# Graph network kernel on one core: source one-hots compared on VectorE, edge-term steps spread singly, features turned early

## The chip, the cores and the metric

The program runs on one core of one Trainium2 chip. The metric is the device time of one execution in microseconds (us), the median over several runs. Names of engines: TensorE (PE, matmuls; PEld is its weight loads), VectorE (DVE), ScalarE (ACT), GpSimd (POOL) and SyncE (SP), which here only issues DMAs.

## The reference, cut to what matters

Four graph layers over 128 nodes with 512 features, each followed by a residual and a layer norm. Only the first two matter here.

```python
# layer 0: attention over the edges, then a feed-forward
h1 = layer_norm(x + attn_out @ Wo + bo)
ff = relu(h1 @ W1 + b1) @ W2 + b2
x  = layernorm(x + layer_norm(h1 + ff))
# layer 1: 4096 edges
edge_feat = concatenate([x[src], x[dst], edge_attr])      # 4096 x (512 + 512 + 64)
h         = mish(edge_feat @ W1 + b1)
messages  = mish(h @ W2 + b2)
agg       = segment_sum(messages, dst, 128)
```

`src` and `dst` are 4096 integers below 128, `edge_attr` is 4096 x 64.

## The kernel before, in words

Every engine has its own instruction stream, written out by hand; semaphores join them. Nothing is scheduled by a tool, so the order in the code is the order on each engine.

The layer-1 product is split. The features of source and destination are first multiplied by W1 per node (128 rows, called Ahi/Alo and Bhi/Blo), and then spread to the edges by a matmul with a one-hot matrix: ST (source) and DT (destination), both 128 nodes x 4096 edges. The third part, `edge_attr @ Wc`, is the edge term: 16 steps, each of two banks of 512 edges, six matmuls (L483) and two evictions on ScalarE (L281) into C. Steps 0 to 11 are the ring steps: they use the four PSUM banks of PRE in turn, so step s waits until ScalarE has evicted step s - 2. Steps 12 to 15 come later, between the matmuls of the first layer (L605).

DT and ST are made in the same way: VectorE compares ids with a row of numbers into Dbf and Sbf (edges on partitions, L825), TensorE turns four tiles of 128 x 128 into a bank (`turn_onehots`, L458), and ScalarE copies the bank out (`onehot_out`, L295), eight groups each. These banks are the same ring as those of the edge term, counted by `pre_done` and `pre_read`. The edge features `ea` are turned too (`turn_features`, L465), in four groups, split into a high part (ScalarE, L313) and a low part (VectorE, L835).

Order of TensorE around the change: scores, values, edge counts; the attention product (L531), Wo (L427, bank1 and bank2), the eight DT groups, the turn of the normed node features (L410), the first feed-forward F1 in four blocks (L436) with two ST groups after each, the second feed-forward F2 (L427) in two halves of six and a last part of four, with edge steps 0, 1-2 and 3-5 between them, then steps 6 to 10, the turn of the next node features (L410), step 11, and the per-node products with W1 (L584 to L589). From there VectorE and ScalarE serve the long edge loop (L605, L622, L632), which is unchanged.

SyncE issues the loads in a fixed order, all on one queue; some wait for a semaphore, because tensors share places in SBUF. VectorE between F1 and the next norm: low part of W1 (L878), `features_low(3)`, two copies of the turned graph matrices (L881, L882), two adds (L885, L887), and then `residual` (L771), which waits for F2's last matmuls and starts a chain of norms that ends with `nx_ready` (L792).

Of the kernel before, what the change touches and what calls it, by code (L numbers as in the profile page):

```python
# [13 lines left out]
N = 128  # L14
D = 512
# [25 lines left out]
def gnn_kernel(nc, a, out):  # L41

    ctx = ExitStack()
    with ctx:
# [33 lines left out]
        def overlay(*spots):  # L78

            made = {}  # L80
            with ExitStack() as st:
                end = 0
                for name, place, units, dt in sorted(spots, key=lambda s: s[1]):
                    if place > end:
# [10 lines left out]
                        ("W1raw", 64, 8, F32), ("EAThi", 72, 4, F32R), ("Wchi", 76, 1, F32R), ("Wc", 77, 1, F32), ("ffT", 78, 2, F32),  # L95
                        ("rows", 80, 7, F32), ("EATlo", 91, 4, F32R))
        other = overlay(("Dbf", 28, 4, BF16), ("Sbf", 52, 4, BF16), ("W1hi", 56, 8, F32R), ("W1lo", 64, 8, F32R),
                        ("Wclo", 77, 1, F32R), ("xhi", 78, 1, F32R), ("xlo", 79, 1, F32R))
        low = overlay(("Clo", 0, 32, F32R), ("Mlo", 64, 4, F32R))
        last = overlay(("W3", 0, 8, F32), ("W4", 8, 4, F32), ("WsR", 12, 4, F32), ("WnR", 16, 4, F32),  # L100
                       ("WsT", 32, 4, F32), ("WnT", 36, 4, F32), ("uT", 40, 1, F32), ("aggT", 41, 1, F32), ("agg_sb", 42, 1, F32),
# [4 lines left out]
        def chunks(v, k):  # L106
            return v.rearrange("p (c n) -> p c n", c=k)
# [11 lines left out]
        C = edge["C"].rearrange("p (g j e) -> p g j e", g=G, j=KC)  # L119
        Hlo, Mlo = low["Clo"].rearrange("p (g j e) -> p g j e", g=G, j=KC), chunks(low["Mlo"], GT)  # L120
        ST, DT = edge["ST"], edge["DT"]
        W2hi, W2lo = chunks(edge["W2hi"], KC), chunks(edge["W2lo"], KC)
        Hhi = edge["Hhi"].rearrange("p (b j e) -> p b j e", b=2, j=KC)
        M, Mhi = chunks(edge["M"], GT), chunks(edge["Mhi"], GT)
# [22 lines left out]
        def quarter(b, j):  # L147
            return b[:, P * j:P * (j + 1)]
# [9 lines left out]

        DT_UNIT, ST_UNIT, C_UNIT = 0, G, 2 * G
        RING_STEPS = KC * (PAIRS - 1)
        UNITS = C_UNIT + 2 * RING_STEPS
        LATE_BANKS = ((bank[3], bank[4]), (bank[1], bank[2]))

        S = {}
        for name in ("x_in ids_in vecs_in ea_in wq_in0 wq_in1 wk_in0 wk_in1 wv_in wo_in f1_in f2_in w1_in wc_in w2_in w3_in w4_in g_in ws_in wn_in b1g_in "
                     "out_stored consts ident_ready ident_bf_ready x_transposed xT_ready cols_done cols_ready q_done k_done v_done "
                     "qk_ready v_ready onehot_bf ct_done ct_read uniform_ready eighth ea_done ea_hi ea_lo wc_hi wc_lo scores_done s_centred exp_done attn_ready ao_done ao_ready wo_done "
                     "stat_ready rstd_ready nx_ready nT_done nT_ready f1_done ff_ready f2_done pre_done pre_read late_done late_read "  # L170
                     "xw_ready w2_hi w2_lo w1_hi w1_lo xs_hi xs_lo ab_done ab_ready "
                     "graphT_ready graphT_done graph_ready deg_ready dinv_ready "
                     "z1_done z1_read h_hi h_lo z2_done z2_read m_hi m_lo m_oh agg_done "
                     "agg_ready aggT_done aggT_ready u_done u_ready o_done "
                     "g0_done g0_ready g1_done g1_ready g2_done g2_ready g3_done nm_done nm_ready l3_done wt_done wt_ready y_final "
                     "dve_chain").split():
            S[name] = sem(name)
# [4 lines left out]
        def w_view(w):  # L182
            return w.rearrange("(c p) n -> p c n", p=P)
# [16 lines left out]
        def _(sp):  # L200
# [13 lines left out]
            for name in EARLY_ROWS[2:4]:  # L214
                load_row(name)
            sp.dma_start(F1, w_view(a["L0_gnn_W1"])).then_inc(S["f1_in"], 16)
            for name in EARLY_ROWS[4:]:
                load_row(name)
            sp.dma_start(W1raw, w_view(a["L1_gnn_W1"][0:2 * D, :])).then_inc(S["w1_in"], 16)

            sp.wait_ge(S["pre_done"], ST_UNIT)
            sp.wait_ge(S["ct_done"], 1)
            sp.dma_start(F2, w_view(a["L0_gnn_W2"])).then_inc(S["f2_in"], 16)
            sp.wait_ge(S["pre_done"], C_UNIT)
            sp.dma_start(W2raw, w_view(a["L1_gnn_W2"])).then_inc(S["w2_in"], 16)


# [42 lines left out]
        def _(act):  # L270
# [22 lines left out]
            def onehot_out(dst, unit, g):  # L293
                act.wait_ge(S["pre_done"], unit + g + 1)
                act.activation(dst[:, GE * g:GE * (g + 1)], PRE[(unit + g) % 4][:, :], ACT.Copy).then_inc(S["pre_read"], 1)  # L295

            def edge_term_out(steps):

                for s in steps:
                    q, j = s // KC, s % KC  # L300
                    for o in range(2):
                        k = 2 * s + o
                        if s < RING_STEPS:
                            act.wait_ge(S["pre_done"], C_UNIT + k + 1)
                            src, signal = PRE[(C_UNIT + k) % 4], "pre_read"
                        else:
                            act.wait_ge(S["late_done"], k - 2 * RING_STEPS + 1)
                            src, signal = LATE_BANKS[s % 2][o], "late_read"
                        bias_out(C[:, 2 * q + o, j, :], src[:, :], "L1_gnn_b1", j).then_inc(S[signal], 1)
# [32 lines left out]
            for i in range(4):  # L342
                w1_high(i)
                relu_out(i)
                onehot_out(ST, ST_UNIT, 2 * i)
                onehot_out(ST, ST_UNIT, 2 * i + 1)
            features_high(3)
            edge_term_out(range(RING_STEPS))
            act.wait_ge(S["w2_in"], 16)
            act.activation(W2hi[:, :, :], W2raw, ACT.Copy).then_inc(S["w2_hi"], 1)  # L350
            edge_term_out(range(RING_STEPS, RING_STEPS + 1))

# [43 lines left out]
        def _(pe):  # L396
# [64 lines left out]
            def turn_features(q):  # L461

                for i in range(GT):
                    t = tile_of(2 * q, i)
                    done = nc.tensor.transpose(quarter(EA_BANKS[q], i), flat(ea[:, t:t + 2, :]), ident[:, :])  # L465
                done.then_inc(S["ea_done"], 1)
# [58 lines left out]
            pe.wait_ge(S["uniform_ready"], 1)  # L525
            for j in range(KC):
                mm(quarter(bank[3], j), v_sb[:, P * j:P * (j + 1)], uniform[:, :], start=j == 0, stop=False)
            for o, j in ((o, j) for o in range(2) for j in range(KC)):
                h = 2 * j + o
                pe.wait_ge(S["attn_ready"], o + 1)  # L530
                done = mm(bank[3][HEAD * o:HEAD * (o + 1), P * j:P * (j + 1)], v_sb[:, HEAD * h:HEAD * (h + 1)], attn[:, o, j, :],  # L531
                          start=False, stop=j == KC - 1)
            done.then_inc(S["ao_done"], 1)
            pe.wait_ge(S["ea_in"], 16)
            turn_features(0)
            pe.wait_ge(S["wo_in"], 16)
            for h in range(2):
                pe.wait_ge(S["ao_ready"], h + 1)
                for b in range(2):
                    done = columns_by((bank[1], bank[2]), aoT, Wo, b, (2 * h, 2 * h + 1), None, KC - 1)  # L540
                    if h == 1:
                        done.then_inc(S["wo_done"], 1)
            pe.wait_ge(S["ident_bf_ready"], 1)
            pe.wait_ge(S["cols_ready"], 1)
            pe.wait_ge(S["ct_read"], 1)
            turn_onehots(Dbf, DT_UNIT, range(G))
            pe.wait_ge(S["ea_lo"], 1)
            turn_features(1)
            transpose_halves((bank[1], bank[2]), y, S["nx_ready"], 0, S["nT_done"])
# [3 lines left out]
            for i in range(4):  # L553
                if i >= 2:
                    pe.wait_ge(S["ea_lo"], 3)
                features_by(F1_BANKS[i], 2 * i, (2 * i, 2 * i + 1), F1, xT, KC, S["f1_done"])
                turn_onehots(Sbf, ST_UNIT, (2 * i, 2 * i + 1))
            pe.wait_ge(S["ff_ready"], FC - 2)
            turn_features(3)
            pe.wait_ge(S["wc_lo"], 1)  # L560
            edge_term(range(1))
            pe.wait_ge(S["f2_in"], 16)
            columns_by((bank[1], bank[2]), ffT, F2, 0, range(FC - 2), 0, FC - 1)
            edge_term(range(1, 3))
            pe.wait_ge(S["graphT_ready"], 2)
            pe.wait_ge(S["ff_ready"], FC)
            nc.tensor.transpose(bank[4][:, 0:N], Ahat[:, :], ident[:, :])
            nc.tensor.transpose(bank[4][:, N:2 * N], Cn[:, :], ident[:, :]).then_inc(S["graphT_done"], 1)
            columns_by((bank[1], bank[2]), ffT, F2, 1, range(FC - 2), 0, FC - 1)
            edge_term(range(3, 6))  # L570
            for h in range(2):
                columns_by((bank[1], bank[2]), ffT, F2, h, range(FC - 2, FC), 0, FC - 1).then_inc(S["f2_done"], 1)

            edge_term(range(6, RING_STEPS - 1))
            pe.wait_ge(S["graph_ready"], 2)
            transpose_halves((bank[3], bank[4]), xs, S["nx_ready"], 2, S["nT_done"])
            edge_term(range(RING_STEPS - 1, RING_STEPS))
# [59 lines left out]
            def turn(q):  # L637
# [5 lines left out]
                    done = nc.tensor.transpose(quarter(TURN[q % 4], k), w[:, k, P * (q % KC):P * (q % KC + 1)], ident[:, :])  # L643
                done.then_inc(S["wt_done"], 1)

            pe.wait_ge(S["ab_ready"], 2)
            first_layer(0, range(3), range(2))
            pe.wait_ge(S["ab_ready"], 6)
# [92 lines left out]
        def _(dve):  # L741
# [91 lines left out]
            def features_low(q):  # L833
                dve.wait_ge(S["ea_hi"], q + 1)
                v.tensor_tensor(EATlo[:, q, :], EA_BANKS[q][:, :], EAThi[:, q, :].bitcast(F32), ALU.subtract).then_inc(S["ea_lo"], 1)  # L835
# [40 lines left out]
            for c in range(2 * KC):  # L876
                dve.wait_ge(S["w1_hi"], c // 2 + 1)
                v.tensor_tensor(W1lo[:, c, :], W1raw[:, c, :], W1hi[:, c, :].bitcast(F32), ALU.subtract).then_inc(S["w1_lo"], 1)  # L878
            features_low(3)
            dve.wait_ge(S["graphT_done"], 1)  # L880
            v.tensor_scalar(Ahat[:, :], bank[4][:, 0:N], small[:, 2:3], None, ALU.mult).then_inc(S["graph_ready"], 1)  # L881
            v.tensor_copy(Cn[:, :], bank[4][:, N:2 * N]).then_inc(S["graph_ready"], 1)  # L882

            dve.wait_ge(S["nx_ready"], 2)
            chain(v.tensor_tensor(xw[:, :], y[:, :], r("L0_gnn_b2"), ALU.add))  # L885
# [142 lines left out]
```

## Time and profile before

| | |
|---|---|
| median of 3 runs | 248.84 us (248.77 to 249.32) |
| the profiled execution | 250.41 us, its span 248.6 us |
| TensorE busy | 233.4 us (94%) |
| VectorE busy | 154.0 us (62%) |
| ScalarE busy | 121.5 us (49%) |
| chain that ended last | PE 82%, DVE 5%, DMA 4%, ACT 4%, issue 2% |

The span counts from the first to the last instruction of the profile; the rest of the profiled execution lies around it. Busy shares are means over stages: here the stretch from 21 to 84 us is what the change touches, and the long edge loop after it (84 to 208 us) keeps TensorE busy without a break.

### The profile page before, as it was taken

What the parts mean: (1) busy time and instruction counts of PE and PEld (TensorE: products, weight loads), DVE (VectorE), ACT (ScalarE), POOL (GpSimd) and SP (SyncE); (2) the same over time, 40 slices, a digit from 0 to 9 for tenths busy, and PEclk for the clock granted to TensorE, in tenths of its full rate; (3) what the DMA queues carried; (4) which work ended last, traced back from release to release, by engine and by line L of the source; (5) the groups of instructions that cost most, each with busy time, mean ns of one, the idle gap of its engine ahead of it and who ended that gap; (6) DMA issues with size and microseconds to landing.
All of it is one profiled execution on the core that took longest, in us unless ns stands there. A gap on an engine that the chain in (4) does not pass through costs nothing.

```text
span 248.6 us, 3285 instructions
## 1 busy us (share of the span) xinstructions
PE 233.4 (94%) x1269; PEld 187.8 (76%) x1269; DVE 154.0 (62%) x266; ACT 121.5 (49%) x221; POOL 5.5 (2%) x17
## 2 busy tenths in 40 slices
PE   7989999998999999999999999999999998999980
PEld 3866779765676788888888888888888887986760
DVE  2959774535669756775855848758567456174724
ACT  0325189857938953654735546456356341260000
POOL 0000000000000000000000000000000000010001
PEclk9999999999999999999999999999999999999997
DMA  7999977400381000008122050040000000000001
GB/s 212 297 400 407 411 261 273 169 4 0 114 255 55 0 0 0 3 0 298 40 80 91 0 170 4 8 161 0 0 3 0 0 0 3 0 0 3 0 0 44
DMA packets 12991, 23.39 MB, mean 94 GB/s; under 512 B 920, under 2 KB 3888, under 8 KB 12848
## 3 DMA queue, kind: packets, MB, share of 16 engines
q1 hardware_dynamic: 12336, 22.81, 25.9%
q10 hardware_dynamic: 640, 0.37, 0.6%
q8 instruction: 10, 0.16, 0.3%
q14 instruction: 5, 0.04, 0.0%
HBM read 22.92 MB, written 0.26 MB: 93 GB/s over the span
## 4 chain that ended last, share of the span: by engine, by line
PE 82%; DVE 5%; DMA 4%; ACT 4%; issue 2%; SPq 1%; POOL 0%; POOLq 0%; DVEq 0%
PE bank L622 33%; PE bank L605 12%; PE bank L427 9%; PE bank L436 6%; DMA Wk<-in_L_gnn_Wk 4%; PE bank L483 4%; PE bank L632 3%; PE bank L633 3%; ACT C L281 2%; PE bank L416 1%; PE bank L643 1%; PE bank L446 1%; PE bank L458 1%; PE bank L410 1%; ACT DT L295 1%
## 5 line engine op out<-in xcount | busy, mean ns | idle before, releaser
L622 PE MATMUL bank<-W2hi,Hhi 128*128 128x512 f32 x128 | 49.8, 389 | 0.0
L622 PE MATMUL bank<-W2lo,Hhi 128*128 128x512 f32 x128 | 49.8, 389 | 0.0
L622 PE MATMUL bank<-W2hi,Clo 128*128 128x512 f32 x128 | 49.8, 389 | 0.0
L365 ACT ACTIVATE Mhi<-M 128x512 fp32r<-128x512 f32 x32 | 20.2, 632 | 45.4 <-DVE M L932 45.4
L937 DVE TENSOR_TENSOR Mlo<-M,Mhi 128x512 fp32r<-128x512 f32 x32 | 22.1, 689 | 24.4 <-ACT M L366 24.4
L932 DVE TENSOR_TENSOR M<-bank,b2r 128x512 f32<-128x512 f32 x32 | 22.0, 687 | 12.7 <-PE bank L633 7.6
L622 PEld LDWEIGHTS bank<-W2lo,Hhi 128*128 128x128 f32 x128 | 24.0, 188 | 5.0
L622 PEld LDWEIGHTS bank<-W2hi,Clo 128*128 128x128 f32 x128 | 24.0, 188 | 5.0
L622 PEld LDWEIGHTS bank<-W2hi,Hhi 128*128 128x128 f32 x128 | 24.0, 188 | 5.0
L358 ACT ACTIVATE Hhi<-C 128x512 fp32r<-128x512 f32 x32 | 20.0, 624 | 12.4 <-DVE C L918 12.1
L918 DVE TENSOR_TENSOR C<-bank,C 128x512 f32<-128x512 f32 x32 | 21.4, 689 | 5.1 <-PE bank L605 4.1
L923 DVE TENSOR_TENSOR Clo<-C,Hhi 128x512 fp32r<-128x512 f32 x32 | 22.0, 687 | 3.7 <-ACT C L359 3.6
L281 ACT ACTIVATE C<-bank,cols 128x512 f32<-128x512 f32 x32 | 19.7, 693 | 9.2 <-PE bank L483 9.2
L605 PE MATMUL bank<-ST,AB 128*128 128x512 f32 x64 | 20.0, 399 | 0.0
L359 ACT ACTIVATE C<-C 128x512 f32<-128x512 f32 x32 | 19.8, 618 | 0.0
L366 ACT ACTIVATE M<-M 128x512 f32<-128x512 f32 x32 | 19.7, 616 | 0.0
L605 PE MATMUL bank<-DT,AB 128*128 128x512 f32 x64 | 19.4, 390 | 0.0
L605 PEld LDWEIGHTS bank<-ST,AB 128*128 128x128 f32 x64 | 11.6, 188 | 3.9 <-DVE C L918 1.0
L605 PEld LDWEIGHTS bank<-DT,AB 128*128 128x128 f32 x64 | 12.0, 188 | 2.6
L632 PE MATMUL bank<-Mhi,Dg 128*128 128x512 f32 x32 | 12.6, 395 | 0.7 <-DVE Mlo L937 0.7
L633 PE MATMUL bank<-Mlo,Dg 128*128 128x512 f32 x32 | 12.5, 389 | 0.0
L446 PE MATMUL bank<-ident 128*128 128x512 bf16 x26 | 8.4, 466 | 1.6 <-DVE ident L819 1.6
(178 smaller groups left out, 316.9 us busy)
## 6 DMA issues: line engine op xcount, KB each, us to landing
F<-in_L_gnn_W SPq DMA_DIRECT2D x2, 2048.0 KB, 13.4
W1raw<-in_L_gnn_W SPq DMA_DIRECT2D x1, 2048.0 KB, 17.6
W<-in_L_gnn_W SPq DMA_DIRECT2D x1, 2048.0 KB, 9.2
Wq<-in_L_gnn_Wq SPq DMA_DIRECT2D x2, 512.0 KB, 5.8
Wk<-in_L_gnn_Wk SPq DMA_DIRECT2D x2, 512.0 KB, 9.7
Wv<-in_L_gnn_Wv SPq DMA_DIRECT2D x1, 1024.0 KB, 12.7
ea<-in_edge_attr SPq DMA_DIRECT2D x1, 1024.0 KB, 12.6
Wo<-in_L_gnn_Wo SPq DMA_DIRECT2D x1, 1024.0 KB, 15.7
```

The source lines that it names most:

```text
L281: return act.activation(dst, src, func, bias=cols[:, col[name] + j:col[name] + j + 1])
L358: act.activation(Hhi[:, g % 2, j, :], C[:, g, j, :], ACT.Mish)
L365: act.activation(Mhi[:, t, :], M[:, t, :], ACT.Mish)
L427: done = mm(banks[h][:, 0:D // 2], lhs[:, c, :], rhs[:, c, D // 2 * h:D // 2 * (h + 1)], start=c == start, stop=c == stop)
L605: done = mm(ST1[u % 3][:, :], w[:, P * j:P * (j + 1)], x[:, GE * g:GE * (g + 1)], start=k == 0, stop=k == len(terms) - 1)
L622: done = mm(ST2[t][:, :], x[:, c, e], w[:, c, :], start=c == 0 and i == 0, stop=c == KC - 1 and i == 2)
L632: mm(AGG[:, :], Dg[:, t, :], Mhi[:, t, :], start=g == 0 and t == 0, stop=False)
L633: done = mm(AGG[:, :], Dg[:, t, :], Mlo[:, t, :], start=False, stop=g == G - 1 and t == GT - 1)
L918: v.tensor_tensor(C[:, g, j, :], ST1[u % 3][:, :], C[:, g, j, :], ALU.add).then_inc(S["z1_read"], 1)
L923: v.tensor_tensor(Hlo[:, g, j, :], C[:, g, j, :], Hhi[:, g % 2, j, :].bitcast(F32), ALU.subtract).then_inc(S["h_lo"], 1)
L932: v.tensor_tensor(M[:, t, :], ST2[t][:, :], row["L1_gnn_b2"], ALU.add).then_inc(S["z2_read"], 1)
L937: v.tensor_tensor(Mlo[:, t, :], M[:, t, :], Mhi[:, t, :].bitcast(F32), ALU.subtract).then_inc(S["m_lo"], 1)
```

## The change

Four things are done together. ST is no longer turned by TensorE and copied by ScalarE: `src` is loaded twice more, each half (2048 ids, 1 MB over all partitions) broadcast to every partition, and VectorE compares it with the partition's number, eight instructions of 4 x 2 x 64 elements. Their input is read with 32 words from one element to the next (innermost), because the ids lie by edge and ST lies by tile. The eight ST groups of `turn_onehots` and `onehot_out` go away. Edge steps 0 to 6 stand singly between the blocks of F1 and F2. `turn_features(0)` and the first DT group move ahead of the attention product. On SyncE's queue three bias rows (L0 b2, g2, be2) move behind F2 and the two id loads, W1raw moves up by those three, and W2raw stands behind them without a wait of its own. ids0 lies where qT, kT, v and aoT were (free when Wo is done), ids1 where AB will be.

```diff
-                        ("Wclo", 77, 1, F32R), ("xhi", 78, 1, F32R), ("xlo", 79, 1, F32R))
+                        ("ids0", 48, 4, I32), ("ids1", 87, 4, I32), ("Wclo", 77, 1, F32R), ("xhi", 78, 1, F32R), ("xlo", 79, 1, F32R))
...
+        ST_by_tile = ST.rearrange("p (q o i s e) -> p q s i o e", q=PAIRS, o=2, i=GT, s=2)
+        row_ids = [other[f"ids{h}"].rearrange("p (e q i o) -> p q i o e", q=PAIRS, o=2, i=GT) for h in range(2)]
...
-        DT_UNIT, ST_UNIT, C_UNIT = 0, G, 2 * G
+        DT_UNIT, C_UNIT = 0, G
...
@@ SyncE
+            sp.dma_start(W1raw, w_view(a["L1_gnn_W1"][0:2 * D, :])).then_inc(S["w1_in"], 16)
+            sp.wait_ge(S["pre_done"], C_UNIT)
+            sp.wait_ge(S["ct_done"], 1)
+            sp.dma_start(F2, w_view(a["L0_gnn_W2"])).then_inc(S["f2_in"], 16)
+            sp.wait_ge(S["wo_done"], 2)
+            for h in range(2):
+                sp.dma_start(other[f"ids{h}"], by_partition(a["src"][E // 2 * h:E // 2 * (h + 1)], E // 2)).then_inc(S[f"row_ids_in{h}"], 16)
             for name in EARLY_ROWS[4:]:
                 load_row(name)
-            sp.dma_start(W1raw, w_view(a["L1_gnn_W1"][0:2 * D, :])).then_inc(S["w1_in"], 16)
-
-            sp.wait_ge(S["pre_done"], ST_UNIT)
-            sp.wait_ge(S["ct_done"], 1)
-            sp.dma_start(F2, w_view(a["L0_gnn_W2"])).then_inc(S["f2_in"], 16)
-            sp.wait_ge(S["pre_done"], C_UNIT)
             sp.dma_start(W2raw, w_view(a["L1_gnn_W2"])).then_inc(S["w2_in"], 16)
@@ ScalarE
             for i in range(4):
                 w1_high(i)
                 relu_out(i)
-                onehot_out(ST, ST_UNIT, 2 * i)
-                onehot_out(ST, ST_UNIT, 2 * i + 1)
+                if i >= 1:
+                    edge_term_out(range(i - 1, i))
             features_high(3)
-            edge_term_out(range(RING_STEPS))
+            edge_term_out(range(3, RING_STEPS))
             act.wait_ge(S["w2_in"], 16)
+            act.wait_ge(S["st_ready"], 2 * PAIRS)
@@ TensorE
+            pe.wait_ge(S["ea_in"], 16)
+            turn_features(0)
+            pe.wait_ge(S["ident_bf_ready"], 1)
+            turn_onehots(Dbf, DT_UNIT, range(1))
             for o, j in ((o, j) for o in range(2) for j in range(KC)):
...
-            turn_onehots(Dbf, DT_UNIT, range(G))
+            turn_onehots(Dbf, DT_UNIT, range(1, G))
...
                 features_by(F1_BANKS[i], 2 * i, (2 * i, 2 * i + 1), F1, xT, KC, S["f1_done"])
-                turn_onehots(Sbf, ST_UNIT, (2 * i, 2 * i + 1))
+                if i == 1:
+                    pe.wait_ge(S["wc_lo"], 1)
+                if i >= 1:
+                    edge_term(range(i - 1, i))
...
+            for h in range(2):
+                columns_by((bank[1], bank[2]), ffT, F2, h, range(0, 3), 0, FC - 1)
+                edge_term(range(2 * h + 3, 2 * h + 4))
+                columns_by((bank[1], bank[2]), ffT, F2, h, range(3, FC - 2), 0, FC - 1)
+                edge_term(range(2 * h + 4, 2 * h + 5))
...
-            edge_term(range(6, RING_STEPS - 1))
+            edge_term(range(7, RING_STEPS - 1))
...
+            pe.wait_ge(S["st_ready"], 2 * PAIRS)
             pe.wait_ge(S["ab_ready"], 2)
             first_layer(0, range(3), range(2))
@@ VectorE
             features_low(3)
+            def source_onehots(h):
+                dve.wait_ge(S[f"row_ids_in{h}"], 16)
+                for q in range(PAIRS):
+                    v.tensor_scalar(ST_by_tile[:, q, h], row_ids[h][:, q], iota_col[:, 0:1], None, ALU.is_equal).then_inc(S["st_ready"], 1)
+            source_onehots(0)
             dve.wait_ge(S["graphT_done"], 1)
             v.tensor_scalar(Ahat[:, :], bank[4][:, 0:N], small[:, 2:3], None, ALU.mult).then_inc(S["graph_ready"], 1)
             v.tensor_copy(Cn[:, :], bank[4][:, N:2 * N]).then_inc(S["graph_ready"], 1)
+            source_onehots(1)
```

TensorE before, from the second half of F1 to the middle of F2 (F<- names either feed-forward weight, ffT is its hidden layer):

```order
L436 MATMUL bank<-xT,F 128x128 x8
L458 MATMUL bank<-ident_bf,Sbf 128x128 x8
L465 MATMUL bank<-ident,ea 128x128 x4
L483 MATMUL bank<-EAThi,Wchi 128x512 x2
L483 MATMUL bank<-EAThi,Wclo 128x512 x2
L483 MATMUL bank<-EATlo,Wchi 128x512 x2
L427 MATMUL bank<-F,ffT 128x256 x6
```

And in the changed kernel at the same place (its lines stand 6 lower in the file):

```order
L442 MATMUL bank<-xT,F 128x128 x8
L489 MATMUL bank<-EAThi,Wchi 128x512 x2
L489 MATMUL bank<-EAThi,Wclo 128x512 x2
L489 MATMUL bank<-EATlo,Wchi 128x512 x2
L471 MATMUL bank<-ident,ea 128x128 x4
L433 MATMUL bank<-F,ffT 128x256 x3
L489 MATMUL bank<-EAThi,Wchi 128x512 x2
L489 MATMUL bank<-EAThi,Wclo 128x512 x2
L489 MATMUL bank<-EATlo,Wchi 128x512 x2
L433 MATMUL bank<-F,ffT 128x256 x3
```

The eight matmuls on Sbf are gone, an edge step stands in their place, and the six of F2 are cut into three and three.

VectorE before, from the low part of W1 to the residual:

```order
L878 TENSOR_TENSOR W1lo<-W1raw,W1hi 128x512 x8
L835 TENSOR_TENSOR EATlo<-bank,EAThi 128x512
L881 TENSOR_SCALAR Ahat<-bank,small 128x128
L882 COPY Cn<-bank 128x128
L885 TENSOR_TENSOR xw<-y,rows 128x512
L887 TENSOR_TENSOR rows<-xs,rows 128x512
L771 TENSOR_TENSOR y<-bank,xw 128x256
```

And in the changed kernel:

```order
L889 TENSOR_TENSOR W1lo<-W1raw,W1hi 128x512 x8
L846 TENSOR_TENSOR EATlo<-bank,EAThi 128x512
L896 TENSOR_SCALAR ST<-ids,iota_col 128x4x2x64 x4
L900 TENSOR_SCALAR Ahat<-bank,small 128x128
L901 COPY Cn<-bank 128x128
L896 TENSOR_SCALAR ST<-ids,iota_col 128x4x2x64 x4
L905 TENSOR_TENSOR xw<-y,rows 128x512
L907 TENSOR_TENSOR rows<-xs,rows 128x512
L782 TENSOR_TENSOR y<-bank,xw 128x256
```

Eight comparisons stand between `features_low(3)` and the residual, four on each side of the graph copies.

## Rows read from the trace of the kernel before

**Rows 1.** Chain that ended last, at 31 us: start, length, work.

```profile
31.71 2.07 ACT DT L295 x4
```

**Rows 2.** Timeline of PE, 24 to 66 us: start, length, idle before and its releaser.

```profile
25.46 1.69 PE L531 MATMUL bank<-attn,MA 128*64 128x128 f32 x16 [1.05 <-DVE attn L854]
...
35.74 2.05 PE L436 MATMUL bank<-xT,F 128*128 128x128 f32 x16 [0.20 <-DVE xT L750]
37.63 0.61 PE L458 MATMUL bank<-ident_bf,Sbf 128*128 128x128 bf16 x8
38.08 2.00 PE L436 MATMUL bank<-xT,F 128*128 128x128 f32 x16
...
49.16 0.49 PE L483 MATMUL bank<-EAThi,Wchi 64*128 64x512 f32 x2
...
50.74 0.33 PE L567 MATMUL bank<-ident,Ahat 128*128 128x128 f32 x1
...
51.02 2.76 PE L427 MATMUL bank<-F,ffT 128*128 128x256 f32 x12
53.70 0.50 PE L483 MATMUL bank<-EAThi,Wchi 64*128 64x512 f32 x2
...
56.12 0.50 PE L483 MATMUL bank<-EAThi,Wchi 64*128 64x512 f32 x2 [0.75 <-ACT C L281]
...
57.02 1.99 PE L427 MATMUL bank<-F,ffT 128*128 128x256 f32 x8
58.94 0.50 PE L483 MATMUL bank<-EAThi,Wchi 64*128 64x512 f32 x2
...
64.62 0.66 PE L410 MATMUL bank<-ident,xs 128*128 128x128 f32 x4
```

**Rows 3.** Timeline of ACT, 37 to 59 us.

```profile
37.45 1.06 ACT L321 ACTIVATE W1hi<-W1raw 128x1024 fp32r<-128x1024 f32 x1 [0.73 <-DMA W1raw<-in_L_gnn_W]
...
47.06 0.72 ACT L313 ACTIVATE EAThi<-bank 128x512 fp32r<-128x512 f32 x1
...
54.71 3.64 ACT L281 ACTIVATE C<-bank,cols 128x512 f32<-128x512 f32 x6 [2.14 <-PE bank L483]
```

**Rows 4.** Timeline of DVE, 33 to 65 us.

```profile
33.37 0.88 DVE L811 SCALAR_TENSOR_TENSOR y<-y,rstd,rows 128x256 f32<-128x256 f32 x2
...
51.22 0.35 DVE L881 TENSOR_SCALAR Ahat<-bank,small 128x128 f32<-128x128 f32 x1 [2.71 <-PE bank L568]
...
51.71 0.69 DVE L885 TENSOR_TENSOR xw<-y,rows 128x512 f32<-128x512 f32 x1
...
58.25 0.43 DVE L771 TENSOR_TENSOR y<-bank,xw 128x256 f32<-128x256 f32 x1 [5.13 <-PE bank L427]
...
63.89 0.73 DVE L792 TENSOR_SCALAR xs<-y,mv,rstd 128x256 f32<-128x256 f32 x2 [0.66 <-POOL rstd L262]
```

**Rows 5.** Groups of VectorE by form, whole span: busy, mean ns, idle before.

```profile
L792 DVE TENSOR_SCALAR xs<-y,mv,rstd 128x256 f32<-128x256 f32 x4 | 1.5, 410 | 1.3 <-POOL rstd L262 1.3
...
L792 DVE TENSOR_SCALAR xs<-bank,mv,rstd 128x256 f32<-128x256 f32 x2 | 1.0, 538 | 0.7 <-POOL rstd L262 0.7
L850 DVE RECIPROCAL total<-total 128x128 f32<-128x128 f32 x1 | 1.0, 953 | 0.0
...
L881 DVE TENSOR_SCALAR Ahat<-bank,small 128x128 f32<-128x128 f32 x1 | 0.4, 352 | 2.7 <-PE bank L568 2.7
```

**Rows 6.** SyncE's queue: DMA issues, start and length of the issue.

```profile
34.26 0.38 SPq L223 DMA_DIRECT2D F<-in_L_gnn_W  x1
```

**Rows 7.** DMA issues of the page: size, median us to landing.

```profile
W2raw<-in_L_gnn_W SPq DMA_DIRECT2D x1, 1024.0 KB, 4.9
```

**Rows 8.** Windows: busy time of each engine, granted clock (PEclk), DMA share, GB/s.

```profile
40.00:42.00 2.00, 2.00 (x24) 2.00 (x23) 1.03 (x2) 2.00 (x5) 0.00 (x0) 1.00 0.89 347
...
240.00:245.00 5.00, 1.25 (x6) 0.76 (x4) 3.52 (x10) 0.00 (x0) 0.60 (x2) 1.00 0.00 2
245.00:248.60 3.60, 0.00 (x0) 0.00 (x0) 0.74 (x2) 0.00 (x0) 0.49 (x1) 0.60 0.22 73
```

More of the change, by code:

```diff
@@ L166, in gnn_kernel @@
         S = {}
-        for name in ("x_in ids_in vecs_in ea_in wq_in0 wq_in1 wk_in0 wk_in1 wv_in wo_in f1_in f2_in w1_in wc_in w2_in w3_in w4_in g_in ws_in wn_in b1g_in "
+        for name in ("x_in ids_in row_ids_in0 row_ids_in1 st_ready vecs_in ea_in wq_in0 wq_in1 wk_in0 wk_in1 wv_in wo_in f1_in f2_in w1_in wc_in w2_in w3_in w4_in g_in ws_in wn_in b1g_in "
                      "out_stored consts ident_ready ident_bf_ready x_transposed xT_ready cols_done cols_ready q_done k_done v_done "
@@ L533, in _ @@
             done.then_inc(S["ao_done"], 1)
-            pe.wait_ge(S["ea_in"], 16)
-            turn_features(0)
             pe.wait_ge(S["wo_in"], 16)
@@ L542, in _ @@
                         done.then_inc(S["wo_done"], 1)
-            pe.wait_ge(S["ident_bf_ready"], 1)
             pe.wait_ge(S["cols_ready"], 1)
             pe.wait_ge(S["ct_read"], 1)
-            turn_onehots(Dbf, DT_UNIT, range(G))
+            turn_onehots(Dbf, DT_UNIT, range(1, G))
             pe.wait_ge(S["ea_lo"], 1)
@@ L556, in _ @@
                 features_by(F1_BANKS[i], 2 * i, (2 * i, 2 * i + 1), F1, xT, KC, S["f1_done"])
-                turn_onehots(Sbf, ST_UNIT, (2 * i, 2 * i + 1))
+                if i == 1:
+                    pe.wait_ge(S["wc_lo"], 1)
+                if i >= 1:
+                    edge_term(range(i - 1, i))
             pe.wait_ge(S["ff_ready"], FC - 2)
             turn_features(3)
-            pe.wait_ge(S["wc_lo"], 1)
-            edge_term(range(1))
             pe.wait_ge(S["f2_in"], 16)
[L563 to L570, printed above, removed]
+            for h in range(2):
[3 more added lines that the diff above has]
+                edge_term(range(2 * h + 4, 2 * h + 5))
+                if h == 0:
+                    pe.wait_ge(S["graphT_ready"], 2)
+                    pe.wait_ge(S["ff_ready"], FC)
+                    nc.tensor.transpose(bank[4][:, 0:N], Ahat[:, :], ident[:, :])
+                    nc.tensor.transpose(bank[4][:, N:2 * N], Cn[:, :], ident[:, :]).then_inc(S["graphT_done"], 1)
             for h in range(2):
                 columns_by((bank[1], bank[2]), ffT, F2, h, range(FC - 2, FC), 0, FC - 1).then_inc(S["f2_done"], 1)
-            edge_term(range(6, RING_STEPS - 1))
+            edge_term(range(7, RING_STEPS - 1))
             pe.wait_ge(S["graph_ready"], 2)
```

## The prediction

> **What bounds it now.** I read first the windows and the chain. After 84 us TensorE runs the edge loop without a break and nothing of it is changed, so only the time at which that loop starts counts. From 31 to 66 us I followed the chain of waits and then the timelines of three engines beside each other. There are three kinds of place. (a) TensorE works and is the bound: F1 and its ST turns, F2. (b) TensorE waits for ScalarE, which evicts banks: four DT evictions stand on the chain for 2.07 us [rows 1], and in the edge steps 3 to 5 TensorE stands still before the third [rows 2]. (c) After F2's last matmul VectorE runs a serial chain from 58.25 us (residual) to 64.62 us (63.89 + 0.73, xs ready) [rows 4]; TensorE turns xs at 64.62 us [rows 2] and then goes on to the per-node products. So the time is set by: when F1 starts, how long it is from F1's start to F2's end, and whether VectorE is free when F2 ends. In the kernel before it has been free for long: it idles 5.13 us ahead of the residual [rows 4].
>
> **Term 1, the turns moved ahead.** TensorE idles 1.05 us before the attention product [rows 2]; `turn_features(0)` and one DT group fit in there (some 0.7 us: the four turns of features that stand elsewhere for 0.45 and half of the 0.45 us of two groups). One of the eight DT evictions is thereby done before the others begin. Four evictions take 2.07 us [rows 1], so TensorE's last group, which waits for the fourth eviction, comes 0.52 us sooner. The turn of y behind it needs y, which VectorE ends at 34.25 us (33.37 + 0.88) [rows 4]; VectorE too is ahead a little, since the first low part of the features can start sooner. I take 0.55 us for the start of F1: 35.74 becomes 35.19. The bound below is 0.3 (y not earlier), above 0.65. ScalarE waited 0.73 us for W1raw [rows 3]; with three bias rows no longer ahead of it that goes, but it was on no chain.
>
> **Term 2, from F1's start to F2's end.** Before: 35.74 to 58.94, 23.2 us [rows 2]. Removed: four times 0.45 us of ST turns (37.63 to 38.08), 1.8. Edge steps before: step 0 alone 0.90, steps 1 and 2 together 1.58 (49.16 to 50.74), steps 3 to 5 together 3.32 (53.70 to 57.02), 5.8 in all; three steps at 0.79 would be 2.4, so 0.9 of it is the wait for ScalarE. After: seven single steps (step 6 now comes before the end of F2), each 0.90 us as the last of the block shows (56.12 to 57.02): 6.3 us. Spread singly they no longer wait: between the starts of two steps lie 2.2 us or more, and the two evictions that free a pair of banks take 1.2 (3.64 for six) [rows 3]. A block of fp32 matmuls behind an edge step costs 0.13 more: eight passes took 1.92 us from 57.02, where twelve behind the graph turns took 2.68 from 51.02 [rows 2], 0.223 each. There are two such blocks before and five after, 0.4 more. Sum: 23.2 - 1.8 - 5.8 + 6.3 + 0.4 = 22.3 us. F2 ends 0.9 us sooner by this, 1.45 with term 1. The residual could start at 58.25 - 1.45 = 56.8 us. Step 6 is not lost work: it leaves only steps 7 to 10 for the time of VectorE's chain, which end near 61.8 us (ScalarE's evictions, 1.2 per step, set them), well before xs.
>
> **Term 3, VectorE's new work.** It must fit between `features_low(3)` and the residual. Edge step 2 starts at 35.19 + four F1 blocks of 1.85 + two steps of 0.90 + twice 0.13 = 44.65. Its first eviction starts 1.01 us later (53.70 and 54.71), two take 1.2, then the high part of the last features 0.72 (the row at 47.06) [rows 2, 3], and the low part 0.6: VectorE comes to the comparisons at 48.1 us. Then eight of them at s each, the graph copies 0.5 (51.22 to 51.71) and two adds of 0.72 [rows 4]: it reaches the residual at 50.0 + 8 s. The place before which nothing is lost is s = 0.85; at s = 1.05 the whole gain is eaten.
>
> What is s? No row shows a VectorE instruction whose input jumps 32 words from one element to the next. Lower bound: a tensor-scalar in SBUF, 256 elements, takes 410 ns, and two follow each other in 0.32 (0.73 less 0.41) [rows 4, 5]; a 512-element instruction follows the next in 0.60 (0.69 less the 0.09 that overlaps), so 0.57 to 0.60. The nearest row of a slower read is the same instruction on a PSUM source: 352 ns for 128 elements, 538 for 256 [rows 5], 1.45 ns an element, which makes 0.91 us for 512. The far end is the reciprocal, 953 ns for 128 [rows 5], over 3 us for 512; nothing speaks for a compare being like it. I take 0.91, a slow read, uncovered by its neighbour. Then VectorE reaches the residual at 57.3 us, 0.5 later than F2 allows and 0.95 earlier than before.
>
> The Trainium skill speaks against the change here, in "Vector Engine (DVE) Microarchitecture Reference", "Measured stream behaviour on trn2": a port streams at full rate only over runs of at least two adjacent words; one source that hops 4 KiB every element costs 1.73 ns an element, and steps of 24 words 2.5. By the first an instruction would be some 0.96 us with its fixed part, and my sum would give about 248.1; by the second 1.36, and about 251.3. No row here shows either.
>
> **Term 4, the end of the chain.** Before, TensorE began to turn xs at 64.62 us, when both halves were out; the first half was ready some 0.35 earlier but TensorE was still in step 10. After, step 10 is long done, the first half is turned early, and only two turns stand behind the second half: 0.2 us more. What follows (step 11, products with W1, first layer) shifts as it is; ScalarE's wait for `st_ready` ahead of W2hi comes at about 65 us, when ST is done.
>
> **DMA.** F2 was issued at 34.26 [rows 6] and its bytes ended before 42 (share 0.89 in 40 to 42, 347 GB/s) [rows 8]; now half a us sooner. A load of 1 MB alone lands in 4.9 us [rows 7], at 347 GB/s 3.0 of it bytes and 1.9 fixed. So ids0 lands near 46.2, ids1 near 49.2, the three bias rows near 51.5, W2raw near 54.5. Needed at 48.1, 52.2, 55.9 and 65: hidden. Without that cover, each us that ids1 comes after 52.2 is lost.
>
> **Sum.** VectorE's 0.95 and 0.2 of term 4: 1.15 us less. On the profiled execution's own 250.41 us that is 249.26; the same difference on the median of the runs, 248.84, gives 247.7 us.
>
> **Rivals.** (1) VectorE fully hidden (s under 0.85): the gain is 1.45 + 0.2 = 1.65, 247.2 us. For it: a 512-element add here takes 0.69 [rows 4]. I count it with the forecast's side, chance 0.25; the forecast itself (s from 0.85 to 0.99) 0.27. (2) The jumping read costs two slots or more per element: 0.60 + 0.53 = 1.13 us each, VectorE reaches the residual at 59.05, 0.8 later than before, less 0.2: 249.4 us; at 1.36 it is 60.9, 251.3 us. TensorE then stands idle from 61.8 until xs, some 5 us; its granted clock was 1.00 over 240 to 245 us with the last work near 241.3, and 0.60 over the stretch behind it [rows 8], so the lower level (1.2 GHz) may be added in that case. It decides from s = 1.12. For it: the ids are read with the jump as their innermost step; against: no row shows that VectorE minds. Chance 0.35. (3) The broadcasts come late. If 1 MB read from the same 8 KB took twice as long, ids1 would land near 55.2 and the residual start near 60.3: 2.05 later, 250.7 us. Against it: ea has the same form, 8 KB to each partition, though from different places; the reference's ids are read from one. Chance 0.03. (4) s between 0.99 and 1.12, no change to be seen, 248.8: 0.10.
>
> **Numbers.** A measurement of this kernel tells about 0.2% (0.5 us) from no change. Faster: 0.25 + 0.27 = 0.52. Within it: 0.10. Slower: 0.35 + 0.03 = 0.38. The forecast's side alone would span 247.0 to 248.3; as rival 2 holds over a third, the range goes up to it: 247.0 to 251.4.
>
> **What would show it.** Right: TensorE without idle before the attention product; F1 starts near 35.2; F2's last block ends near 57.5; no wait of TensorE for ScalarE in steps 0 to 6; eight comparisons of 0.9 us and a residual near 57.3 with no or little idle before it. Wrong: comparisons of 1.2 us or more, VectorE waiting for ids, a residual later than 58.25, or an F2 that waits for its weights.

## The result, and the profile after

| | before | changed |
|---|---|---|
| median | 248.9 us (248.75 to 249.32, 7 runs) | 247.71 us (247.54 to 248.35, 7 runs) |
| profiled execution, span | 250.41, 248.6 us | 247.65, 245.9 us |

The ratio is 0.9949, with a 95% interval of 0.9937 to 0.9961: 1.27 us faster (0.97 to 1.57). The forecast was 247.7 us. (One execution of a kernel named below, "one-hots alone", took 391 us at a granted clock of 0.56 and is in no number of this text.)

The spans of the two profiled executions differ by 2.7 us, more than twice as much. The timeline of TensorE in the changed kernel says why (start, length, work, idle before it and its releaser):

```profile
24.24 1.69 PE L541 MATMUL bank<-attn,MA 128*64 128x128 f32 x16 [0.40 <-DVE attn L865]
26.53 3.69 PE L433 MATMUL bank<-Wo,MA 128*128 128x256 f32 x16 [0.61 <-DVE MA L868]
...
34.02 3.84 PE L442 MATMUL bank<-xT,F 128*128 128x128 f32 x32 [0.19 <-DVE xT L761]
37.79 0.49 PE L489 MATMUL bank<-EAThi,Wchi 64*128 64x512 f32 x2
...
38.68 2.05 PE L442 MATMUL bank<-xT,F 128*128 128x128 f32 x16
...
54.55 1.99 PE L433 MATMUL bank<-F,ffT 128*128 128x256 f32 x8
56.47 0.50 PE L489 MATMUL bank<-EAThi,Wchi 64*128 64x512 f32 x2
...
61.98 0.67 PE L416 MATMUL bank<-ident,xs 128*128 128x128 f32 x4 [0.97 <-DVE xs L803]
...
80.94 0.40 PE L632 MATMUL bank<-W2hi,Hhi 128*128 128x512 f32 x1
```

The attention product (the first row) starts 1.22 us sooner than in [rows 2] (25.46). The change is not the cause: its two early turns do stand ahead of that product, but in both kernels the product starts 2.11 us after the matmuls with `uniform` before it (23.35 and 25.46 before, 22.13 and 24.24 after), held by VectorE's attn. So the stretches are compared from there. F1 starts 9.78 us after the attention product (before 10.28). F2 ends 22.45 us after F1's start (before 23.20); its end is read as the start of the edge step behind it. The turn of xs starts 5.51 us after F2's end (before 5.68). With what follows, the edge loop starts 56.70 us after the attention product. In the kernel before it was 58.17: 1.47 us less, inside the interval of the timed runs.

The timeline of VectorE in the changed kernel, answering to [rows 4]:

```profile
46.94 2.44 DVE L896 TENSOR_SCALAR ST<-ids,iota_col 128x512 fp32r<-128x512 int32 x4
50.08 0.35 DVE L900 TENSOR_SCALAR Ahat<-bank,small 128x128 f32<-128x128 f32 x1 [0.70 <-PE bank L580]
...
50.54 2.42 DVE L896 TENSOR_SCALAR ST<-ids,iota_col 128x512 fp32r<-128x512 int32 x4
52.88 0.68 DVE L905 TENSOR_TENSOR xw<-y,rows 128x512 f32<-128x512 f32 x1
...
55.78 0.42 DVE L782 TENSOR_TENSOR y<-bank,xw 128x256 f32<-128x256 f32 x1 [1.49 <-PE bank L433]
...
61.42 0.73 DVE L803 TENSOR_SCALAR xs<-y,mv,rstd 128x256 f32<-128x256 f32 x2 [0.67 <-POOL rstd L267]
```

And the group of the comparisons (busy, mean ns):

```profile
L896 DVE TENSOR_SCALAR ST<-ids,iota_col 128x512 fp32r<-128x512 int32 x8 | 4.9, 670 | 0.0
```

They follow each other in 0.60 us, not in 0.91, and VectorE idles 1.49 us ahead of the residual, released by TensorE. So VectorE's new work is hidden. The end of F2 sets when the residual starts, and VectorE's chain of norms from there sets when TensorE can turn xs.

### The profile page after: what moved, and what is told of

Its sections match the earlier page's. It is cut to its first block, busy times and chain, and to the rows that moved or that the text cites. A ratio compares the mean times of both kernels' runs of the same rounds, so it can differ in the third digit from the quotient of the medians.

```text
span 245.9 us, 3224 instructions
## 1 busy us (share of the span) xinstructions
PE 231.3 (94%) x1237; PEld 185.1 (75%) x1237; DVE 158.6 (65%) x274; ACT 118.0 (48%) x213; POOL 5.6 (2%) x17
## 4 chain that ended last, share of the span: by engine, by line
PE 80%; DVE 7%; DMA 5%; issue 3%; ACT 2%; SPq 1%; POOL 1%; POOLq 0%; DVEq 0%
PE bank L632 33%; PE bank L615 12%; PE bank L433 8%; PE bank L442 6%; DMA Wv<-in_L_gnn_Wv 5%; PE bank L489 4%; PE bank L642 3%; PE bank L643 3%; PE bank L422 2%; PE bank L653 1%; PE bank L452 1%; PE bank L416 1%; PE bank L594 1%; DVE M L952 1%; PE bank L595 1%
```

## The experiments

Eleven further runs were made: the two kernels of above once more each, and nine kernels that differ from them in one piece or a few. Ahead of each result stands what was expected of it: what theory A says, and what its rival B. The stretches in the table are differences between starts of rows of TensorE's timeline, in us: from the attention product to F1, from F1 to F2's end, from there to the turn of xs, and from the attention product to the edge loop. Beside these runs the kernel before was timed again, at 248.83 to 248.88 us; ratios are to it.

| kernel | median | to F1 | F1 to F2's end | to the turn of xs | to the edge loop |
|---|---|---|---|---|---|
| before | 248.9 | 10.28 | 23.20 | 5.68 | 58.17 |
| before, again | 248.83 | 10.28 | 23.19 | 5.68 | 58.12 |
| changed | 247.71 | 9.78 | 22.45 | 5.51 | 56.70 |
| changed, again | 247.63 | 9.78 | 22.46 | 5.50 | 56.72 |
| turns back | 247.83 | 10.27 | 22.47 | 5.50 | 57.21 |
| turns early alone | 248.30 | 9.78 | 23.19 | 5.70 | 57.62 |
| one-hots alone | 246.97 | 10.27 | 21.24 | 5.70 | 56.19 |
| step 6 behind | 246.64 | 9.79 | 21.37 | 5.68 | 55.86 |
| steps grouped | 246.37 | 9.78 | 21.24 | 5.68 | 55.73 |

**The kernel before, again** (no edit).

> The kernel before, unchanged, as a second look. The two profiles differ in something the change does not touch: the attention product starts at 25.46 us before and at 24.24 after, so 1.22 us of the 2.7 us between the spans lies ahead of the change. Theory A (that is only how the first loads fell in the two executions): time equal to before within 0.1%, and in this profile the attention product may start anywhere between 24.0 and 25.5, while the length from there to the start of the edge loop (L622) stays at 58.17 us within 0.1. Rival B (the order of the later DMA issues sets when the first weights land): the attention product starts near 25.4 here too.

Ratio 1.0001 (0.999 to 1.0013). The attention product started at 23.99 us here, against 25.46 in the first profile; from there to the edge loop the length was 58.12, the same within 0.05. So theory A: the early difference is that of one execution's first loads, and no part of the change. In the first profile TensorE waits for two of them (Wq 0.23 us, Wk 0.73), in this one for neither, and ends the products with Wk at 14.06 us instead of 15.75. The longer wait:

```profile
13.70 2.05 PE L436 MATMUL bank<-xT,Wk 128*128 128x128 f32 x16 [0.73 <-DMA Wk<-in_L_gnn_Wk]
```

**Turns back** (the changed kernel):

```diff
-            pe.wait_ge(S["ea_in"], 16)
-            turn_features(0)
-            pe.wait_ge(S["ident_bf_ready"], 1)
-            turn_onehots(Dbf, DT_UNIT, range(1))
             for o, j in ((o, j) for o in range(2) for j in range(KC)):
...
-            turn_onehots(Dbf, DT_UNIT, range(1, G))
+            turn_onehots(Dbf, DT_UNIT, range(G))
```

> The changed kernel with the turn of features 0 and of the first DT group back behind the attention product. Theory A: F1 starts 0.50 us later after the attention product than in the changed kernel (10.28 instead of 9.78), the rest shifts, 0.5 us slower than the changed kernel. Rival B (the early turns are hidden by VectorE's norm of y): no difference within 0.1 us.

The trace shows theory A to within a hundredth (F1 10.27 us after the attention product, against 9.78). The medians, 247.83 and 247.71, alone would not: the ratio to before is 0.9955 (0.9939 to 0.9972), and 0.5 us more than the changed kernel's 0.9949 would be 0.9969, just inside. The attention product started at 23.76 here and at 24.24 in the changed kernel, which by itself hides 0.48 us between these two profiles.

**Turns early alone** (the kernel before with the same four lines moved ahead).

> The kernel before with only the two turns moved early. Theory A: 0.5 us faster than before, F1's start 9.8 us after the attention product. Rival B: no more than 0.1 us.

Ratio 0.9976 (0.9964 to 0.9989), 0.53 us faster, F1 9.78 us after the attention product. Theory A. The loads stand in their old order here, so the 0.50 us come from the turns and not from W1raw's earlier load.

**Step 6 behind** (the changed kernel):

```diff
-                edge_term(range(2 * h + 4, 2 * h + 5))
+                if h == 0:
+                    edge_term(range(4, 5))
...
-            edge_term(range(7, RING_STEPS - 1))
+            edge_term(range(6, RING_STEPS - 1))
```

> The changed kernel with edge step 6 behind the last part of F2, where it stood before. Theory A (VectorE's serial chain after F2 is the bound, and TensorE stood idle 0.97 us in it): F2 ends 1.03 us sooner (0.90 for the step, 0.13 for the block behind it), VectorE has 1.49 us of slack to take it, the five steps 6 to 10 end near 61.0 by ScalarE's evictions and xs is ready near 61.1; 0.85 to 1.0 us faster than the changed kernel. Rival B (ScalarE's five evictions then set the turn of xs, as in the kernel before): 0.3 us faster or less, with an idle of TensorE released by ScalarE directly ahead of the turn of xs.

Ratio 0.9903 (0.9885 to 0.9921). The median is 1.07 us below the changed kernel's; in the trace the edge loop starts 0.84 us sooner. F2 ended 21.37 us after F1's start, 1.08 sooner. TensorE's rows ahead of the turn of xs, and VectorE's row of xs:

```profile
60.17 0.50 PE L489 MATMUL bank<-EAThi,Wchi 64*128 64x512 f32 x2 [0.25 <-ACT C L286]
...
61.07 0.65 PE L416 MATMUL bank<-ident,xs 128*128 128x128 f32 x4
```

```profile
60.34 0.74 DVE L804 TENSOR_SCALAR xs<-y,mv,rstd 128x256 f32<-128x256 f32 x2 [0.67 <-POOL rstd L267]
```

VectorE had xs at 61.08 (60.34 + 0.74), and TensorE, held by ScalarE's evictions, came to the turn at 61.07, with no idle time: the two chains are now equally long, as in the kernel before. In the changed kernel TensorE could start to turn the first half of xs 0.17 us before the second was out (61.98 against 61.42 + 0.73 = 62.15); here it cannot. So theory A gave the size, and the evictions that B named are there too and take back a part: of the 1.08 us at F2's end, 0.84 are left at the edge loop.

**Ids in order** (the changed kernel):

```diff
-        row_ids = [other[f"ids{h}"].rearrange("p (e q i o) -> p q i o e", q=PAIRS, o=2, i=GT) for h in range(2)]
+        row_ids = [other[f"ids{h}"].rearrange("p (q i o e) -> p q i o e", q=PAIRS, o=2, i=GT) for h in range(2)]
```

> The changed kernel with the ids read in the order in which they lie (one run of 512 words per instruction) instead of with 32 words between elements; ST then holds other edges, so the output is not the reference's. Theory A (the jump costs nothing on this source): the instruction takes 0.67 us here too and the time is that of the changed kernel. Rival B (in order it would run at twice the rate, so the jump does cost something that is hidden by 1.49 us of slack): 0.41 us or less per instruction, the time still the same.

247.49 us, ratio 0.9939 (0.9925 to 0.9953): the time of the changed kernel. Its group of comparisons:

```profile
L896 DVE TENSOR_SCALAR ST<-ids,iota_col 128x512 fp32r<-128x512 int32 x8 | 3.3, 480 | 0.0
```

480 ns against 670: the jump of 32 words does cost, 0.19 us an instruction, 1.5 us in all, and all of it is hidden. Theory A falls for the instruction. B's 0.41 was too low for the length of one; from one to the next it is 0.40 (four took 1.67), against 0.60 with the jump. Both had the time.

**Comparisons twice** (the changed kernel):

```diff
+                    chain(v.tensor_scalar(ST_by_tile[:, q, h], row_ids[h][:, q], iota_col[:, 0:1], None, ALU.is_equal))
                     v.tensor_scalar(ST_by_tile[:, q, h], row_ids[h][:, q], iota_col[:, 0:1], None, ALU.is_equal).then_inc(S["st_ready"], 1)
```

> The changed kernel with each comparison done twice, one behind the other with a semaphore between: about 1.3 us per pair, near the price that the prediction gave for a jumping read at its worst. Theory A (residual reached at the start of the comparisons plus 8 s plus 1.94): VectorE reaches the residual near 59.4 instead of 55.78, 3.6 us slower than the changed kernel and 2.3 slower than before. Rival B (some of it is hidden still, or VectorE's work is not on the path): less than 1.5 us slower than the changed kernel. If TensorE's clock falls in the longer idle time, the loss is above 4 us and the granted clock of the stretch behind shows it.

253.67 us, ratio 1.0181 (1.016 to 1.0202): 5.96 us slower than the changed kernel. VectorE reached the residual at 59.23 and did not wait there, as theory A says:

```profile
59.23 0.42 DVE L782 TENSOR_TENSOR y<-bank,xw 128x256 f32<-128x256 f32 x1
```

The rest is the clock. Its windows show the busy time of PE, PEld, DVE, ACT and POOL, then the granted clock, DMA share and GB/s:

```profile
60.00:63.00 3.00, 0.96 (x6) 0.52 (x6) 2.79 (x7) 2.23 (x4) 0.55 (x1) 1.00 0.00 0
63.00:65.40 2.40, 0.00 (x0) 0.01 (x1) 1.64 (x6) 0.00 (x0) 0.55 (x1) 0.91 0.00 0
65.40:68.00 2.60, 2.58 (x10) 1.54 (x10) 2.08 (x7) 0.00 (x0) 0.00 (x0) 0.50 0.32 107
68.00:70.00 2.00, 2.00 (x7) 1.60 (x6) 0.29 (x1) 1.88 (x3) 0.00 (x0) 0.50 1.02 271
70.00:72.00 2.00, 2.00 (x7) 1.57 (x6) 0.00 (x0) 1.18 (x1) 0.00 (x0) 0.55 1.02 360
72.00:75.00 3.00, 3.00 (x15) 2.47 (x14) 2.15 (x4) 0.00 (x0) 0.00 (x0) 1.00 0.76 186
```

TensorE's row of the turn:

```profile
65.42 1.09 PE L416 MATMUL bank<-ident,xs 128*128 128x128 f32 x4 [4.45 <-DVE xs L803]
```

TensorE stood idle 4.45 us ahead of it; the clock fell to its lower level (1.2 GHz) some 0.45 us before this row starts and stayed there until about 71.8. From the turn of xs to the edge loop it took 21.84 us (65.42 to 87.26) where the changed kernel takes 18.96 (61.98 to 80.94): 2.9 us of the loss. The turn itself started 3.5 us later, counted from the attention product. Together 6.4; the medians differ by 5.96.

**Second half twice** (the line above only for `h == 1`).

> The changed kernel with each comparison of the second half done twice, those of the first half once. Theory A (the loss is VectorE's late arrival at the residual alone until TensorE's idle time grows as long as it was with all comparisons twice): VectorE comes to the residual near 57.2 instead of 55.78, TensorE is idle some 2.4 us ahead of the turn of xs, the granted clock stays at 1.00, and the kernel is 1.4 us slower than the changed one. Rival B (the clock falls in an idle time of 2.4 us too): the stretch behind shows 0.5 and the loss is above 3 us.

250.48 us, ratio 1.0077 (1.0057 to 1.0098): 2.85 us slower than its neighbour on the same chip. The arrival was theory A's (residual at 56.93, the turn of xs 39.17 us after the attention product against 37.74, 1.43 later). The clock was rival B's. The row of TensorE and the windows behind it:

```profile
63.13 0.67 PE L416 MATMUL bank<-ident,xs 128*128 128x128 f32 x4 [2.39 <-DVE xs L803]
```

```profile
63.00:63.50 0.50, 0.37 (x3) 0.34 (x4) 0.31 (x1) 0.00 (x0) 0.00 (x0) 1.00 0.00 0
63.50:65.00 1.50, 1.50 (x10) 0.72 (x10) 1.42 (x5) 0.07 (x1) 0.00 (x0) 0.77 0.24 82
65.00:66.00 1.00, 1.00 (x3) 0.81 (x4) 0.66 (x2) 1.00 (x2) 0.00 (x0) 0.50 0.77 252
66.00:67.00 1.00, 1.00 (x4) 0.81 (x3) 0.00 (x0) 1.00 (x2) 0.00 (x0) 0.50 1.06 311
67.00:68.00 1.00, 1.00 (x4) 0.77 (x4) 0.00 (x0) 1.00 (x1) 0.00 (x0) 0.63 0.97 195
68.00:69.00 1.00, 1.00 (x6) 0.81 (x5) 0.00 (x0) 0.00 (x0) 0.00 (x0) 1.00 0.95 328
```

An idle time of 2.39 us was enough, and the clock fell only after TensorE was at work again, at about 64.3. It cost 1.57 us (20.53 from the turn of xs to the edge loop, against 18.96), as much as the 1.43 us that the turn came later. The loss that B gave, above 3, was a little too high; theory A's 1.4 was half of what was measured.

**Ids ahead of F2** (the changed kernel: the loop over the two id loads stands ahead of F2's two waits and its load).

> The changed kernel with the two loads of ids issued ahead of F2's weights. Theory A (one queue, served in order): F2's 2 MB start some 5.5 us later, land near 47.7 instead of 42.1, and TensorE waits for them from about 45, 2.5 to 3 us slower than the changed kernel. Rival B (the queue's transfers share the engines, so the order of issue matters little): under 0.5 us.

247.50 us, ratio 0.9947 (0.993 to 0.9964): no loss. The time is rival B's, but the order did matter: F2 landed later. The DMA issues of the changed kernel and of this one:

```profile
32.54 0.37 SPq L224 DMA_DIRECT2D F<-in_L_gnn_W  x1
32.95 1.63 SPq L227 DMA_DIRECT2D ids<-in_src  x2
```

```profile
30.27 0.82 SPq L224 DMA_DIRECT2D ids<-in_src  x2
32.56 0.38 SPq L227 DMA_DIRECT2D F<-in_L_gnn_W  x1
```

The ids wait for Wo alone and so went out 2.3 us before F2 could be (F2 still waits for the DT groups). The queue stood nearly empty there in the changed kernel (69 GB/s in 32 to 34 us). F2 landed 12.2 us after its issue, at 44.8, where in the changed kernel it took 9.6 us and landed at 42.1; it was needed at 45.0. So F2 came 2.7 us later and not the 5.6 that theory A gave, and still in time, with 0.2 us to spare. That the half-empty queue is what made up the difference is a reading of the two traces; what a later F2 would cost was not tried. (In this one profile the granted clock is 0.95 throughout, so its stretches are not in the table.)

**Steps grouped** (the changed kernel with the edge steps of the kernel before):

```diff
-                if i >= 1:
-                    edge_term(range(i - 1, i))
...
+            edge_term(range(1))
             pe.wait_ge(S["f2_in"], 16)
...
+            columns_by((bank[1], bank[2]), ffT, F2, 0, range(FC - 2), 0, FC - 1)
+            edge_term(range(1, 3))
...
+            columns_by((bank[1], bank[2]), ffT, F2, 1, range(FC - 2), 0, FC - 1)
+            edge_term(range(3, 6))
...
-            edge_term(range(7, RING_STEPS - 1))
+            edge_term(range(6, RING_STEPS - 1))
```

ScalarE's evictions are grouped in the same way.

> The changed kernel with the edge steps in the places of the kernel before (0, then 1 and 2, then 3 to 5, then 6 to 10 behind F2); source one-hots on VectorE and the early turns stay. Theory A (spreading the steps removes the wait of 0.9 us, but costs 0.4 in blocks behind an edge step and 0.9 for step 6): F1's start to F2's end is 23.2 - 1.8 = 21.4 us instead of 22.45, and this kernel is 0.8 to 1.0 us faster than the changed one, the same as the one with step 6 behind. Rival B (spreading is what brings the gain): 0.5 us slower than the changed kernel or more.

Ratio 0.99 (0.9884 to 0.9915), 246.37 us, the lowest median of all. Between the medians it is 1.34 us faster than the changed kernel, in the trace 0.97. Theory A: F1's start to F2's end is 21.24 us, and the wait for ScalarE in steps 3 to 5 is back:

```profile
49.58 0.51 PE L487 MATMUL bank<-EAThi,Wchi 64*128 64x512 f32 x2
...
50.40 0.40 PE L487 MATMUL bank<-EAThi,Wchi 64*128 64x512 f32 x2
...
52.00 0.50 PE L487 MATMUL bank<-EAThi,Wchi 64*128 64x512 f32 x2 [0.75 <-ACT C L286]
...
52.89 2.00 PE L431 MATMUL bank<-F,ffT 128*128 128x256 f32 x8
```

Even with it, F2 ends sooner than with step 6 ahead of it, and 0.13 us sooner than with single steps and step 6 behind (21.37). So of the 0.97 us that the changed order of the steps costs, step 6 makes 0.84, and spreading the other six 0.13. VectorE waited 0.80 us for ids0 here, since its work ahead of the comparisons was done sooner; that is hidden too: it still idled 2.85 us ahead of the residual.

**One-hots alone** (steps grouped and turns back).

> Of the change only the source one-hots on VectorE and the loads that go with them; the edge steps and the turns stand where they stood before. Theory A: TensorE loses the 1.8 us of ST turns and nothing is given back, so 1.8 to 1.9 us faster than before (246.95), 0.5 slower than the kernel with grouped steps and early turns. Rival B (the early turns are worth only 0.1 us once ST is gone, as the two times with and without them seemed to say): 0.1 slower than that kernel, 246.5.

246.97 us, ratio 0.9917 (0.9904 to 0.993): 1.91 us below the neighbouring runs of before (248.88). In the trace the edge loop starts 1.98 us sooner, and 1.96 of that lie between F1's start and F2's end. Theory A. The ST turns themselves took 1.79 us before; the other 0.16 are F1's own blocks, which took 7.41 us with the turns between them and take 7.25 one behind another (33.58 to 40.83 in the kernel with grouped steps). That sum leaves nothing for the new order of the loads, which is part of this kernel too. The early turns are worth 0.46 us in the trace (56.19 against 55.73) and 0.60 between the medians.

**The changed kernel, again** (no edit).

> The changed kernel once more, on the same chip as the two above, as their neighbour: 247.5 to 247.8, and from the attention product to the start of the edge loop 56.7 us within 0.1.

Ratio 0.9945 (0.9933 to 0.9958), 56.72 us. It repeats.

## Why the prediction was right, step by step

Term 1, the turns moved ahead: 0.55 forecast, 0.50 in the trace, shown by moving them alone, forth and back.

Term 2, from F1's start to F2's end: 22.3 forecast, 22.45 measured, so 0.75 gained and not 0.9. The single steps cost 0.89 to 0.90 each as assumed, and an F1 block behind an edge step 0.14 more (1.98 or 1.99 instead of 1.84). The two six-pass blocks of F2 that don't stand behind an edge step took 0.05 more than by 0.223 a pass (1.39 instead of 1.34). In all, the blocks of F1 and F2 grew by 0.6 us and not by 0.4. No step waited for ScalarE before F2's end, as forecast.

What the text did not say is what the sum itself holds. Spreading takes away the wait of 0.9 us but makes each step dearer, so six steps go only from 5.8 to 5.4; against these 0.4 stand 0.9 for step 6 and 0.4 for the blocks. The new order of the steps takes away 1.0 us of the 1.9 to 2.0 that the one-hots give. "Step 6 is not lost work" is the sentence that failed: it was reasoned that it relieves the time after F2, but there TensorE ends idle for 0.97 us, and with step 6 back behind F2 the edge loop starts 0.84 us sooner.

Term 3, VectorE: this step was wrong in its number, and with it the mechanism of the forecast. I took s = 0.91 us by the slope of a PSUM read; it is 0.60 (670 ns, less the overlap with the next), about the lower bound of the text. One part of the error needed no run: 0.91 is the length of one instruction, and the overlap of 0.09 that the lower bound allows for was not taken off; with it s would have been 0.82, below the 0.85 at which VectorE is hidden. So VectorE was not 0.5 us late but 1.49 early, and of the forecast's cases rival 1 (VectorE fully hidden, 247.2 us) is the mechanism that held. By it and the sizes of terms 1, 2 and 4 the gain would be 1.65; the trace gives 1.47. That the forecast of 1.15 met the measured 1.27 is luck. The wrong s took 0.5 us off the gain, and the gain of a hidden VectorE was itself put 0.18 too high (term 2 by 0.15, term 1 by 0.05, term 4 by 0.03, less 0.05 gained behind the turn of xs). The medians alone (0.97 to 1.57) would even have spoken for the forecast's case and against the 1.65; only the idle time ahead of the residual tells the two apart. The form for VectorE's arrival was right: the form 50.0 + 8 s, started 1.2 us earlier by this profile's earlier attention product, puts VectorE at the residual at 53.6 with s = 0.60, and it was free at 54.29 (53.60 + 0.69; 0.70 us of that is its wait for the graph turns). With all comparisons doubled (1.30 us a pair) it gives 59.2, and VectorE came at 59.23.

The rule that I set against the change ("Vector Engine (DVE) Microarchitecture Reference", "Measured stream behaviour on trn2" of the Trainium skill: full rate only over runs of at least two adjacent words) agrees in sign, since the ids in order took 480 ns and with the jump 670. Its 1.73 ns an element, measured there on a two-source program and 0.96 us an instruction by my estimate, does not hold for this one-source instruction, which took 0.67. Its 2.5 for steps of 24 words stands there for both sources at once or for the output, not for one source.

Term 4: 0.2 forecast, 0.17 measured, with the first half of xs no longer kept waiting; step 6 ahead of F2 is what bought it (5.68 again without). DMA: the ids landed at about 44.6 and 47.0 us, before their use at 46.94 and 50.54. Moved to the first profile's time that is 45.8 and 48.2, 0.4 and 1.0 us sooner than forecast.

Of the signs that the text named as right, these came: F1's start (35.24 by the first profile's time), F2's end (57.7), no wait for ScalarE in steps 0 to 6. These did not: TensorE still idles 0.40 us before the attention product, the comparisons are of 0.67 us, and VectorE idles ahead of the residual.

The price of rival 2 left the clock out, as something that may be added. By its form a kernel with s = 1.30 takes 250.8 us; with the comparisons at 1.30 us a pair it took 253.67, and 2.9 us of that is the clock. The text named the fall of the clock for an idle time of some 5 us; 2.39 us sufficed here.

## What to carry to other kernels

Work that fills another engine's idle time is free only up to the place where it would have been needed, and a step moved ahead of a serial chain must save more behind it than it costs in front: ask which engine waits at the end of the chain before moving anything ahead of it. Take one change apart into its pieces even when the whole is faster: here one piece gave 1.9 us, one 0.5, and one took back 1.0. A forecast that meets the time isn't yet shown by it: look for the wait or idle time that tells its case from the rival's. Compare profiles from a common event behind the first loads, since two executions of one kernel differed by 1.5 us before anything of interest began.

## What the runs showed of the hardware that was not expected

After an idle time of TensorE of 2.39 us its granted clock went from 1.00 to 0.50 for some 3.4 us, and the fall came 1.2 us after the work had begun again; after 4.45 us it was down when the work began, for over 6 us of it. With 0.97 and 1.06 us of idle time it stayed at 1.00. So the 1.4 us by which the turn of xs came later with the second half doubled cost 1.6 us more in clock. Idle times between 1.06 and 2.39 us were not tried.

A VectorE compare of 512 int32 with a scalar took 480 ns with its input in order and 670 ns with 32 words between elements. Why the one in order is shorter than the 690 ns of a two-source add of 512 elements was not tried.
